# Routing of the third and fourth batch placed between the first units of a mixture-of-experts feed-forward

## The chip, the cores and the metric

The kernel runs on one core of a Trainium2 chip. The metric is the device time of one execution in microseconds; the time shown for a kernel is the median of its runs. The engines are TensorE (PE, matmuls), VectorE (DVE), ScalarE (ACT), GpSimd (POOL) and the sync engine (SP), which here issues most DMAs. Each engine has its own queue of instructions, which it works in order; engines wait for one another by semaphores (`wait_ge(semaphore, value)`, `then_inc(semaphore, 1)`).

## The reference

The input x is 4 batches of 512 tokens with 128 channels. Four blocks follow, each added to x with a tanh gate: a dynamic-time-warping alignment with a context, a first feed-forward, attention to the context, a second feed-forward. The change lies in the first feed-forward, a mixture of 64 experts of width 64 with 8 chosen for each token:

```python
logits = jnp.einsum('bsh,he->bse', hidden_states, router_w)
affinity = jax.nn.sigmoid(logits)
top_scores, top_idx = jax.lax.top_k(affinity, K)                       # K = 8
top_w = top_scores / (jnp.sum(top_scores, axis=-1, keepdims=True) + 1e-09)
...
shared = jnp.einsum('bsi,ih->bsh', jax.nn.silu(hidden_states @ shared_gate_w) * (hidden_states @ shared_up_w), shared_down_w)
...
expert_act = jax.nn.silu(gate_out) * up_out
routed = jnp.einsum('bsei,eih->bsh', expert_act * router_mask[..., None], expert_down_k)
return shared + routed
```

## The kernel before

**Tiling.** The program works with the hidden width on the partitions and the tokens on the free side, a chunk of 512 tokens (one batch) at a time. The experts are taken in 33 groups of 128 rows: group 0 is the shared expert, each further group holds two routed experts. A unit is one group and one chunk; unit u = 4 * group + chunk, so units 0 to 3 are the shared expert (no mask), 4 to 7 group 1, and unit 8 is the first of group 2. Every fp32 operand is split in a high and a low part, and each product is three matmuls of 128x512 (high x high, low x high, high x low).

**One unit.** TensorE makes the gate product (lines 1203 to 1205, tile `bank`, ps[4] or ps[5]) and the up product (same lines, tile `bank_pair`, ps[6] or ps[7]); ScalarE takes the silu of the gate (L1017); VectorE multiplies silu and up (L1901 for the shared expert; L1903 and then L1911, with the mask, for the others) and counts the semaphore `act`; ScalarE rounds the result to act_hi (L1003); GpSimd subtracts it to get act_lo (L803); TensorE makes the down product, L1356 and L1357 with act_hi and L1359 with act_lo. TensorE's order is gate(u), up(u), down(u - 2). Gate(u) waits for the silu of unit u - 2, up(u) for the `act` of unit u - 2 (it overwrites that unit's bank), L1359 for act_lo. ScalarE's order is silu(u), act_hi(u - 1). GpSimd's L803 waits for act_hi. The first three groups are written out in the program, the others run in loops.

**Routing.** For each batch b, TensorE makes the logits and ScalarE the sigmoid (L988, its semaphore `s_score`). VectorE's `route0(b)` finds the 8 best scores of each of the 4 tiles (L1698), their sum (L1700), the scores with the best replaced by 0 (L1702), and the reciprocal of the sum (L1704, L1706); that releases `s_rcp`. GpSimd's `route0(b)` subtracts to leave the 8 chosen scores (L789) and multiplies by the reciprocal (L793, two instructions); that releases `s_sel`. VectorE's `turn0(b)` transposes the weights (L1711) and releases `s_wt`.

**Masks.** The sync queue waits for `s_wt` in `store_masks0(b)` and writes the weights of batch b to DRAM with 4 DMAs (L634). `mask0` reads them back, each row copied to 64 partitions, with 2 DMAs (L610): for group 1 batch by batch, for the later groups all four batches in one pair. The order in its queue is: store 0; then for b = 0 to 3: store b + 1, wait for store b, load the mask of group 1 for batch b; then the pair of group 2 (tile `mask`, buffer 0), which VectorE's L1911 of unit 8 waits for; then a loop that loads the weights of group g and, once all units of group g - 2 are done on VectorE, the mask of group g.

```python
sp.wait_ge(s_upd, B)
store_masks0(0)
for b in range(B):
    if b + 1 < B:
        store_masks0(b + 1)
    sp.wait_ge(s_mst[b], 16 * 4)
    mask0(1, 1, slice(b, b + 1), s_mask1[b])
mask0(2, 0, slice(0, B), FF_MASK[0][0])
```

In the kernel before, VectorE runs route0 of all four batches and turn0 of the first three ahead of unit 0, and turn0(3) ahead of unit 1; GpSimd runs route0 of all four batches ahead of its unit 0. Most of the tiles named here lie in one large tensor, which the profile calls `arena`.

Of the kernel before, what the change touches and what calls it, by code (L numbers as in the profile page):

```python
# [36 lines left out]
def program(nc, x, ctx_1024, g_xattn, g_ffn, r0_w, sg0, su0, sd0, eg0, eu0, ed0,  # L37
            Wq, bq, Wk, bk, Wv, bv, Wo, bo, r1_w, wg1, wu1, wd1, swg1, swu1, swd1, out):
    B, S, H = x.shape
# [83 lines left out]
    with ctx:  # L123
# [229 lines left out]
        def mask_loaded(half):  # L353

            return 16 * MASK_DMAS * half

        def products(f, u):

            return u - CHUNKS * SHARED[f]
# [324 lines left out]
        def _(pool):  # L684
# [100 lines left out]
            def route0(b):  # L785

                tiles = slice(TPB * b, TPB * (b + 1))
                pool.wait_ge(s_rcp, b + 1)
                nc.gpsimd.tensor_tensor(rest[0][:, tiles, :], aff[0][:, tiles, :], rest[0][:, tiles, :],  # L789
                                        ALU.subtract).then_inc(s_dif, 1)  # L790
                pool.wait_ge(s_dif, b + 1)
                for k in range(2):
                    ins = nc.gpsimd.tensor_tensor(wsel[0][:, b, TPB * k:TPB * (k + 1), :], rest[0][:, tiles, 32 * k:32 * (k + 1)],  # L793
                                                  rsum[:, 2, tiles].unsqueeze(2).broadcast_to([P, TPB, 32]), ALU.mult)
                ins.then_inc(s_sel, 1)

            def feed_forward(f):
                def unit(g, k):
                    u = CHUNKS * g + k
                    pool.wait_ge(FF[f]["ahi"], u + 1)  # L800
                    if not (isinstance(g, int) and u < 2):
                        pool.wait_ge(FF[f]["down"], u - 1)
                    nc.gpsimd.tensor_tensor(act_lo[:, k % 2, :], act_a[:, k % 2, :], act_hi[:, k % 2, :].bitcast(F32),  # L803
                                            ALU.subtract).then_inc(FF[f]["alo"], 1)

                for u in range(CHUNKS * PEEL):
                    if f == 0 and u == 0:
                        for b in range(B):
                            route0(b)
                    unit(u // CHUNKS, u % CHUNKS)  # L810
                with pool.Fori(0, LOOPS[f]) as t:
                    for u in range(BODY * CHUNKS):
                        unit(BODY * t + PEEL + u // CHUNKS, u % CHUNKS)
                for u in range(CHUNKS * (GROUPS[f] - REST), CHUNKS * GROUPS[f]):
                    unit(u // CHUNKS, u % CHUNKS)

            norm(1)
            feed_forward(0)
            norm(2)
            attention()  # L820
            norm(3)
            feed_forward(1)


# [605 lines left out]
        def _(dve):  # L1430
            steps = [0]

            def done(ins):

                steps[0] += 1
                ins.then_inc(s_dve, 1)
                return steps[0]

            def after(step):

                dve.wait_ge(s_dve, step)
# [38 lines left out]
            def low(k, b):  # L1480
                dve.wait_ge(s_xhi, B * k + b + 1)
                nc.vector.tensor_tensor(xn_lo[:, sl(b)], xT[:, sl(b)], xn_hi[:, sl(b)].bitcast(F32),
                                        ALU.subtract).then_inc(s_xlo, 1)
# [209 lines left out]
            def route0(b):  # L1693

                tiles = slice(TPB * b, TPB * (b + 1))
                dve.wait_ge(s_score, b + 1)
                for t in range(TILES)[tiles]:
                    best = done(nc.vector.max(top8[:, t, :], aff[0][:, t, :]))  # L1698
                after(best)
                total = done(nc.vector.tensor_reduce(rsum[:, 0, tiles], top8[:, tiles, :], AX_X, ALU.add))  # L1700
                for t in range(TILES)[tiles]:
                    done(nc.vector.match_replace(rest[0][:, t, :], top8[:, t, :], aff[0][:, t, :], 0.0))  # L1702
                after(total)
                total = done(nc.vector.tensor_scalar(rsum[:, 1, tiles], rsum[:, 0, tiles], 1e-9, None, ALU.add))  # L1704
                after(total)
                nc.vector.reciprocal(rsum[:, 2, tiles], rsum[:, 1, tiles]).then_inc(s_rcp, 1)  # L1706

            def turn0(b):

                dve.wait_ge(s_sel, b + 1)  # L1710
                nc.vector.transpose(wT[0][:, b].rearrange("p t c -> p (t c)"),  # L1711
                                    wsel[0][:, b].rearrange("p t c -> p (t c)")).then_inc(s_wt, 1)
# [170 lines left out]
            def feed_forward(f):  # L1883
                def split_lo(g, j):

                    dve.wait_ge(FF[f]["whi"], g + 1)
                    nc.vector.tensor_tensor(w_lo[:, j, :], w_raw[:, j, :], w_hi[:, j, :].bitcast(F32),  # L1887
                                            ALU.subtract).then_inc(FF[f]["wlo"], 1)

                def unit(g, k, j, half, last=False):  # L1890
                    u = CHUNKS * g + k
                    i = k % 2
                    early = isinstance(g, int) and u < 2
                    if k == SPLIT_AT and not last and not (isinstance(g, int) and g == 0):
                        split_lo(g + 1, 1 - j)
                    dve.wait_ge(FF[f]["silu"], u + 1)
                    dve.wait_ge(FF[f]["up"], u + 1)
                    if isinstance(g, int) and g < SHARED[f]:
                        if not early:
                            dve.wait_ge(FF[f]["alo"], u - 1)  # L1900
                        nc.vector.tensor_tensor(act_a[:, i, :], act_s[:, i, :], ps[6 + i][:], ALU.mult).then_inc(FF[f]["act"], 1)  # L1901
                        return
                    nc.vector.tensor_tensor(ps[6 + i][:], act_s[:, i, :], ps[6 + i][:], ALU.mult).then_inc(FF[f]["t"], 1)  # L1903
                    if f == 0 and isinstance(g, int) and g == 1:
                        dve.wait_ge(s_mask1[k], 16 * MASK_DMAS)
                    elif k == 0:
                        dve.wait_ge(FF_MASK[f][j], mask_loaded(half))
                    dve.wait_ge(FF[f]["t"], products(f, u + 1))
                    if not early:
                        dve.wait_ge(FF[f]["alo"], u - 1)  # L1910
                    nc.vector.tensor_tensor(act_a[:, i, :], ps[6 + i][:], mask[:, j, 512 * k:512 * (k + 1)],  # L1911
                                            ALU.mult).then_inc(FF[f]["act"], 1)

                for g in range(PEEL):
                    for k in range(CHUNKS):
                        u = CHUNKS * g + k
                        if f == 0 and u == 0:

                            route0(0)
                            for b in range(1, B):  # L1920
                                route0(b)
                                turn0(b - 1)
                        if f == 0 and u == 1:
                            turn0(B - 1)
                        if f == 1 and u == 2:
                            low(3, B - 1)
                        if f == 1 and u in ROUTE1_BEFORE:
                            for part, step in ROUTE1_BEFORE[u]:
                                route1(part, step)
                        unit(g, k, g % 2, g // 2)  # L1930
                with dve.Fori(0, LOOPS[f]) as t:
                    for i in range(BODY):
                        for k in range(CHUNKS):
                            unit(BODY * t + PEEL + i, k, (PEEL + i) % 2, BODY // 2 * t + (PEEL + i) // 2)
                for g in range(GROUPS[f] - REST, GROUPS[f]):
                    for k in range(CHUNKS):
                        unit(g, k, g % 2, g // 2, last=g == GROUPS[f] - 1)

            norm(1, add_aligned)
            feed_forward(0)  # L1940
            norm(2, add_ffn(0))
            attention()
            feed_forward(1)
            for n in range(CHUNKS):
                add_ffn(1)(n)
# [26 lines left out]
```

## Time and profile before

| | |
|---|---|
| median of 3 runs | 762.02 us (761.12 to 763.22) |
| profiled execution | 759.99 us, span 758.3 us |
| busy, share of span | PE 87%, DVE 75%, ACT 52%, POOL 46% |
| first feed-forward's units | from about 146 us to about 430 us |
| mean granted TensorE clock | 0.903 of full speed |

The span runs from the first to the last recorded instruction of the profiled execution. PE is TensorE's matmuls, and the sync queue is shown as SPq. In a timeline, the figure in brackets is the time that the engine stood idle before the instruction, followed by what released it. Busy shares are means over all stages; what an edit is worth is read in its own stage.

### The profile page before, as it was taken

What the parts mean: (1) busy time and instruction counts of PE and PEld (TensorE: products, weight loads), DVE (VectorE), ACT (ScalarE), POOL (GpSimd) and SP (SyncE); (2) the same over time, 40 slices, a digit from 0 to 9 for tenths busy, and PEclk for the clock granted to TensorE, in tenths of its full rate; (3) what the DMA queues carried; (4) which work ended last, traced back from release to release, by engine and by line L of the source; (5) the groups of instructions that cost most, each with busy time, mean ns of one, the idle gap of its engine ahead of it and who ended that gap; (6) DMA issues with size and microseconds to landing.
All of it is one profiled execution on the core that took longest, in us unless ns stands there. A gap on an engine that the chain in (4) does not pass through costs nothing.

```text
span 758.3 us, 13278 instructions
## 1 busy us (share of the span) xinstructions
PE 656.2 (87%) x3528; PEld 502.7 (66%) x3528; DVE 570.3 (75%) x1608; ACT 397.4 (52%) x707; POOL 349.5 (46%) x326
## 2 busy tenths in 40 slices
PE   5329523889999999999999779988989999999997
PEld 2116313667888888888888546655768888888885
DVE  6579895857777777777777784889867777777775
ACT  4624220555655655565556544544456555655654
POOL 4000130565666666666666560000356666666664
PEclk9855555699999999999999968998799999999999
DMA  6565543067776776677677100000166656665761
GB/s 155 76 86 169 166 131 62 7 147 151 161 145 139 159 154 141 146 157 154 135 154 158 28 2 2 2 2 13 38 122 153 151 133 160 156 144 138 159 153 56
DMA packets 85148, 86.50 MB, mean 114 GB/s; under 512 B 41109, under 2 KB 65294, under 8 KB 82166
## 3 DMA queue, kind: packets, MB, share of 16 engines
q1 hardware_dynamic: 77340, 79.80, 49.4%
q10 hardware_dynamic: 7769, 6.25, 3.1%
q8 instruction: 17, 0.28, 0.1%
q14 instruction: 22, 0.17, 0.1%
HBM read 76.84 MB, written 9.17 MB: 113 GB/s over the span
## 4 chain that ended last, share of the span: by engine, by line
PE 71%; DVE 12%; DMA 5%; issue 4%; SPq 4%; ACT 2%; POOL 2%; ACTq 1%; DVEq 0%; POOLq 0%
PE bank L1203 7%; PE bank L1204 7%; PE bank_quad L1359 7%; PE bank L1205 7%; PE bank_pair L1203 7%; PE bank_quad L1356 7%; PE bank_pair L1204 7%; PE bank_pair L1205 7%; PE bank_quad L1357 7%; DMA scr_d<-arena 3%; PE bank_pair L1252 2%; PE bank L1295 2%; DVE arena L1670 1%; PE bank_pair L1175 1%; DVE rden L1799 1%
## 5 line engine op out<-in xcount | busy, mean ns | idle before, releaser
L803 POOL TENSOR_TENSOR act_lo<-arena,act_hi 128x512 fp32r<-128x512 f32 x232 | 300.3, 1294 | 191.2 <-ACT act_hi L1003 147.7
L1017 ACT ACTIVATE arena<-bank 128x512 f32<-128x512 f32 x232 | 138.8, 598 | 183.3 <-PE bank L1205 183.3
L1903 DVE TENSOR_TENSOR bank_pair<-arena,bank_pair 128x512 f32<-128x512 f32 x220 | 152.4, 693 | 99.9 <-ACT arena L1017 70.6
L1911 DVE TENSOR_TENSOR arena<-bank_pair,arena 128x512 f32<-128x512 f32 x220 | 152.1, 691 | 17.8 <-DMA arena<-scr_mask 5.7
L1003 ACT ACTIVATE act_hi<-arena 128x512 fp32r<-128x512 f32 x232 | 144.5, 623 | 14.4 <-DVE arena L1901 7.5
L1359 PE MATMUL bank_quad<-act_lo,w_hi 128*128 128x512 f32 x232 | 93.0, 401 | 4.0 <-POOL act_lo L803 4.0
L1203 PE MATMUL bank_pair<-xn_hi,w_hi 128*128 128x512 f32 x232 | 92.8, 400 | 3.5 <-DVE arena L1911 1.8
L1203 PE MATMUL bank<-xn_hi,w_hi 128*128 128x512 f32 x232 | 93.1, 401 | 0.0
L1204 PE MATMUL bank<-xn_hi,w_lo 128*128 128x512 f32 x232 | 93.1, 401 | 0.0
L1356 PE MATMUL bank_quad<-act_hi,w_hi 128*128 128x512 f32 x232 | 93.0, 401 | 0.0
L1204 PE MATMUL bank_pair<-xn_hi,w_lo 128*128 128x512 f32 x232 | 92.1, 397 | 0.0
L1357 PE MATMUL bank_quad<-act_hi,w_lo 128*128 128x512 f32 x232 | 91.4, 394 | 0.0
L1205 PE MATMUL bank<-xn_lo,w_hi 128*128 128x512 f32 x232 | 91.4, 394 | 0.0
L1205 PE MATMUL bank_pair<-xn_lo,w_hi 128*128 128x512 f32 x232 | 91.3, 394 | 0.0
L748 POOL TENSOR_SCALAR xn<-x_res,mv,rstd 128x128 f32<-128x128 f32 x16 | 14.1, 884 | 116.5 <-DVE rstd L1466 81.5
L1175 PE MATMUL bank_pair<-ident,prep_in 128*128 128x128 f32 x75 | 21.6, 425 | 41.2 <-ACT prep_out L953 30.5
L1359 PEld LDWEIGHTS bank_quad<-act_lo,w_hi 128*128 128x128 f32 x232 | 43.7, 189 | 18.1 <-POOL act_lo L803 7.1
L1203 PEld LDWEIGHTS bank_pair<-xn_hi,w_hi 128*128 128x128 f32 x232 | 44.1, 190 | 15.8 <-DVE arena L1911 2.6
L1887 DVE TENSOR_TENSOR w_lo<-w_raw,w_hi 128x384 fp32r<-128x384 f32 x54 | 52.4, 970 | 0.0
L1203 PEld LDWEIGHTS bank<-xn_hi,w_hi 128*128 128x128 f32 x232 | 44.3, 191 | 11.0 <-issue 1.9
L1204 PEld LDWEIGHTS bank<-xn_hi,w_lo 128*128 128x128 f32 x232 | 44.3, 191 | 10.4
L1205 PEld LDWEIGHTS bank_pair<-xn_lo,w_hi 128*128 128x128 f32 x232 | 44.2, 190 | 10.6
(252 smaller groups left out, 981.1 us busy)
## 6 DMA issues: line engine op xcount, KB each, us to landing
arena<-scr_mask SPq DMA_DIRECT2D x94, 512.0 KB, 6.6
scr_w<-prep_out ACTq DMA_DIRECT2D x25, 192.0 KB, 2.4
w_raw<-scr_w SPq DMA_DIRECT2D x25, 192.0 KB, 6.3
w_raw<-in_L_ffn_expert_gate_k SPq DMA_DIRECT2D x32, 64.0 KB, 5.9
w_raw<-in_L_ffn_expert_up_k SPq DMA_DIRECT2D x32, 64.0 KB, 5.6
w_raw<-in_L_ffn_expert_down_k SPq DMA_DIRECT2D x64, 32.0 KB, 5.3
prep_in<-in_L_ffn_wg SPq DMA_DIRECT2D x21, 64.0 KB, 2.0
prep_in<-in_L_ffn_wu SPq DMA_DIRECT2D x21, 64.0 KB, 2.4
```

The lines of the kernel that those rows point to most:

```text
L803: nc.gpsimd.tensor_tensor(act_lo[:, k % 2, :], act_a[:, k % 2, :], act_hi[:, k % 2, :].bitcast(F32), ALU.subtract).then_inc(FF[f]["alo"], 1)
L1003: nc.scalar.activation(act_hi[:, j, :], act_a[:, j, :], ACT.Copy).then_inc(FF[f]["ahi"], 1)
L1017: nc.scalar.activation(act_s[:, k % 2, :], ps[4 + k % 2][:], ACT.Silu).then_inc(FF[f]["silu"], 1)
L1203: nc.tensor.matmul(out, w_h, x_h, start=start, stop=False)
L1204: nc.tensor.matmul(out, w_l, x_h, start=False, stop=False)
L1205: return nc.tensor.matmul(out, w_h, x_l, start=False, stop=stop)
L1356: nc.tensor.matmul(ps[n][:], w_hi[:, j, DOWN:DOWN + P], act_hi[:, i, :], start=first, stop=False)
L1357: nc.tensor.matmul(ps[n][:], w_lo[:, j, DOWN:DOWN + P], act_hi[:, i, :], start=False, stop=False)
L1359: nc.tensor.matmul(ps[n][:], w_hi[:, j, DOWN:DOWN + P], act_lo[:, i, :], start=False, stop=last).then_inc(FF[f]["down"], 1)
L1887: nc.vector.tensor_tensor(w_lo[:, j, :], w_raw[:, j, :], w_hi[:, j, :].bitcast(F32), ALU.subtract).then_inc(FF[f]["wlo"], 1)
L1903: nc.vector.tensor_tensor(ps[6 + i][:], act_s[:, i, :], ps[6 + i][:], ALU.mult).then_inc(FF[f]["t"], 1)
L1911: nc.vector.tensor_tensor(act_a[:, i, :], ps[6 + i][:], mask[:, j, 512 * k:512 * (k + 1)], ALU.mult).then_inc(FF[f]["act"], 1)
```

## The change

VectorE: ahead of unit 0 stand only route0(0), route0(1) and turn0(0). Ahead of unit 1 stand route0(2) and turn0(1), ahead of unit 2 route0(3) and turn0(2), ahead of unit 3 turn0(3). GpSimd: ahead of unit 0 stand route0(0) and route0(1), ahead of unit 1 route0(2), ahead of unit 2 route0(3). No instruction, tile, semaphore or DMA is added or removed, and the programs of TensorE, ScalarE and the sync engine stay as they are.

```diff
@@ GpSimd, feed_forward
                 for u in range(CHUNKS * PEEL):
-                    if f == 0 and u == 0:
-                        for b in range(B):
+                    if f == 0 and u < B - 1:
+                        for b in (range(2) if u == 0 else (u + 1,)):
                             route0(b)
                     unit(u // CHUNKS, u % CHUNKS)
@@ VectorE, feed_forward
                         if f == 0 and u == 0:
-
                             route0(0)
-                            for b in range(1, B):
-                                route0(b)
-                                turn0(b - 1)
-                        if f == 0 and u == 1:
-                            turn0(B - 1)
+                            route0(1)
+                            turn0(0)
+                        if f == 0 and 1 <= u < B:
+                            if u + 1 < B:
+                                route0(u + 1)
+                            turn0(u)
```

## Rows read from the trace of the kernel before

**Rows 1.** The page: chain that ended last, shares of the span by engine.

```profile
PE 71%; DVE 12%; DMA 5%; issue 4%; SPq 4%; ACT 2%; POOL 2%; ACTq 1%; DVEq 0%; POOLq 0%
```

**Rows 2.** TensorE's timeline, 138 to 182 us: start, length, line, tiles, [idle before, releaser].

```profile
148.67 0.63 PE L1205 MATMUL bank_pair<-xn_lo,w_hi 128*128 128x512 f32 x1
...
151.08 0.39 PE L1203 MATMUL bank<-xn_hi,w_hi 128*128 128x512 f32 x1
...
153.68 0.50 PE L1203 MATMUL bank_pair<-xn_hi,w_hi 128*128 128x512 f32 x1 [1.76 <-DVE arena L1901]
...
155.71 0.51 PE L1359 MATMUL bank_quad<-act_lo,w_hi 128*128 128x512 f32 x1 [0.60 <-POOL act_lo L803]
...
162.31 0.39 PE L1203 MATMUL bank<-xn_hi,w_hi 128*128 128x512 f32 x1
...
170.66 0.39 PE L1203 MATMUL bank<-xn_hi,w_hi 128*128 128x512 f32 x1
...
174.52 0.39 PE L1203 MATMUL bank<-xn_hi,w_hi 128*128 128x512 f32 x1
```

**Rows 3.** Waits, 140 to 175 us (total, times, longest); last the sync queue's.

```profile
DVE arena L1911 <- DMA arena<-scr_mask: 2.6, 1, 2.6
...
SPq L634 <- DVE arena L1711: 0.2, 1, 0.2
```

**Rows 4.** Timeline of VectorE, 120 to 215 us, same columns.

```profile
148.43 0.41 DVE L1711 STREAM_TRANSPOSE arena<-arena 128x256 f32<-128x256 f32 x1
148.77 0.56 DVE L1698 MAX8 arena<-arena 128x8 f32<-128x64 f32 x4
...
150.53 0.42 DVE L1711 STREAM_TRANSPOSE arena<-arena 128x256 f32<-128x256 f32 x1
...
152.98 0.65 DVE L1901 TENSOR_TENSOR arena<-arena,bank_pair 128x512 f32<-128x512 f32 x1
154.40 0.45 DVE L1711 STREAM_TRANSPOSE arena<-arena 128x256 f32<-128x256 f32 x1 [0.77 <-POOL arena L793]
...
171.40 0.69 DVE L1911 TENSOR_TENSOR arena<-bank_pair,arena 128x512 f32<-128x512 f32 x1 [2.57 <-DMA arena<-scr_mask]
```

**Rows 5.** Timeline of GpSimd, 138 to 182 us.

```profile
152.80 0.72 POOL L789 TENSOR_TENSOR arena<-arena 128x256 f32<-128x256 f32 x1 [0.53 <-DVE arena L1706]
153.60 0.76 POOL L793 TENSOR_TENSOR arena<-arena 128x128 f32<-128x128 f32 x2
154.37 1.28 POOL L803 TENSOR_TENSOR act_lo<-arena,act_hi 128x512 fp32r<-128x512 f32 x1
```

**Rows 6.** Timeline of ScalarE, 138 to 182 us.

```profile
150.58 0.60 ACT L1017 ACTIVATE arena<-bank 128x512 f32<-128x512 f32 x1 [1.62 <-PE bank L1205]
```

**Rows 7.** The sync queue's timeline, 138 to 182 us, issues merged.

```profile
148.92 3.85 SPq L634 DMA_DIRECT2D scr_mask<-arena  x8
152.82 1.11 SPq L610 DMA_DIRECT2D arena<-scr_mask  x2
...
156.12 2.10 SPq L610 DMA_DIRECT2D arena<-scr_mask  x2
...
160.38 3.75 SPq L610 DMA_DIRECT2D arena<-scr_mask  x6
```

**Rows 8.** The same, narrow stretches at 150.8, 156.7 and 163.8 us.

```profile
150.98 0.32 SPq L634 DMA_DIRECT2D scr_mask<-arena  x1
...
156.64 1.59 SPq L610 DMA_DIRECT2D arena<-scr_mask  x1
...
163.51 0.62 SPq L610 DMA_DIRECT2D arena<-scr_mask  x1
```

**Rows 9.** DMAs issued at 161.0 and 163.6 us: KB, us to landing.

```profile
arena<-scr_mask SPq DMA_DIRECT2D x1, 128.0 KB, 3.3
...
arena<-scr_mask SPq DMA_DIRECT2D x1, 512.0 KB, 7.9
```

**Rows 10.** One stretch: busy PE, PEld, DVE, ACT, POOL; clock, DMA share, GB/s.

```profile
240.00:280.00 40.00, 40.00 (x174) 32.21 (x173) 30.54 (x44) 23.40 (x43) 24.96 (x20) 1.00 0.73 147
```

## The prediction

> **What bounds the kernel now.** The first view to read is the chain of work that ended last [rows 1]: 71% of the span lies on TensorE, so a microsecond moves the end only where TensorE waits for it. Inside the loop of the first feed-forward there is no such wait: a stretch of 40 us shows TensorE busy for 40.00 us [rows 10]. A delay at the loop's entry is therefore never made up in it, and a gain there would be kept. The change touches only that entry, 144 to 158 us, so the timelines of that stretch come next.
>
> TensorE there works through steps. Step u is the gate product of unit u, its up product, and the down product of unit u - 2 (nine matmuls, then the next step). The first matmuls (L1203) of steps 6 and 10 start at 162.31 and 170.66, so a step takes (170.66 - 162.31) / 4 = 2.09 us [rows 2]. Three things interrupt this rhythm [rows 2]. The up product of step 2 waits 1.76 us, to 153.68, because it overwrites a bank that VectorE's unit 0 must have read. The down product of unit 0 waits 0.60 us for GpSimd's act_lo. And step 11 starts at 174.52 instead of at 170.66 + 2.09 = 172.75, 1.77 us late. This third loss begins on VectorE: its multiplication by the mask of group 2 (unit 8) waits 2.57 us for the DMA of the mask, to 171.40 [rows 4], the only DMA wait of any engine in this stretch [rows 3]. The first two losses are what routing costs at the entry; the third is the price of the masks that routing produces.
>
> **Why both are one question.** VectorE's transpose turn0(b) ends the routing of batch b, and the sync queue stores the batch right after it. The queue starts at 148.92, just behind turn0(0) at 148.43 [rows 4, 7]. Its fifth store starts at 150.98, when turn0(1), started at 150.53 and 0.42 long, has ended; the queue waited only 0.2 us for it [rows 3, 4, 8]. From then on it is a row of issues almost without a gap up to 163.51, where the second half of the mask of group 2 is issued [rows 7, 8]; that half lands 7.9 us later, at 171.4 [rows 9], where VectorE's wait ends. The queue's own issuing carries the length from 150.98 to 171.4, so whatever delays the fifth store delays the landing.
>
> **The change, part 1: VectorE's unit 0 comes earlier.** No instruction is added or removed and no DMA is moved in the program. Unit 0 (L1901) now follows turn0(0). It needs the up product, whose last matmul starts at 148.67 and takes 0.63 [rows 2]; so it starts at 149.4 instead of 152.98 and ends at 150.0 [rows 4]. TensorE's up product of step 2 needs it at 151.8, so the 1.76 us go.
>
> What is late next is GpSimd. ScalarE's act_hi of unit 0 stands behind its silu of unit 1 (150.58, 0.60 long [rows 6]), so it runs from 151.1 to 151.7, and act_lo of unit 0 runs on GpSimd from 151.8 to 153.05 (1.28 [rows 5]). Without the gap TensorE reaches that point at 152.9 and waits 0.2. Then GpSimd works its own queue in order. A route0 costs it from 152.80 to 153.60 + 0.76 = 154.36, so 1.56 us [rows 5]. Route0(2) takes it to 154.6, act_lo of unit 1 to 155.9, route0(3) to 157.5, act_lo of unit 2 to 158.8. TensorE wants act_lo of unit 1 at 155.3 and of unit 2 at 158.2: two waits of 0.7. Step 2 starts at 151.08 [rows 2], before any of this; four steps take 8.36 us, the three waits 1.6, and the refilling of the pipeline after each some 0.1, which puts step 6 at 161.3 instead of 162.31. The entry alone gains 1.0 us.
>
> **Part 2: VectorE's routing comes later.** Route0(2) started at 148.77 and its turn0(1) at 150.53, 1.76 later [rows 4]. It now starts behind unit 0, at 149.95. Turn0(1) starts at 151.7 and ends at 152.15, and the fifth store starts at 152.2 instead of 150.98: 1.2 us later. The next stores, those of batch 2, follow four stores and two mask loads: from 150.98 to the end of those loads at 152.82 + 1.11 = 153.93 are 2.95 us [rows 7, 8], so the queue is free for them at 155.15. Turn0(2) must wait for GpSimd's route0(2), to 154.65, and ends at 155.05, 0.1 ahead of that. Turn0(3) stands behind GpSimd's route0(3) at 157.5 and ends at 157.95; the queue wants it four stores and two loads later (4 x 0.48 + 2.10 [rows 7]), at 159.2. Both keep pace, so the queue is 1.2 us late throughout. VectorE itself waits 1.8 us for that last transpose, as it already waits 0.77 for it now [rows 4]; unit 3 behind it ends at 158.6, and the up product of step 5 wants it at 159.9. This costs nothing.
>
> **Part 3: where the two meet.** The masks of group 1 come first. The second half of batch 2's pair lands 3.3 us after its issue [rows 9], at 164.2 now and at 165.4 after. Unit 6, ready at 164.1 by the earlier start, must wait for it, and its act_lo then ends at 168.2, where TensorE wanted it at 167.4: 0.9 of the 1.0 us gained is gone before step 9. By that reckoning step 10 starts at 170.7, as before the change. Then the mask of group 2 lands at 171.4 + 1.2 = 172.6. Everything behind it (the second product of unit 8, act_hi, act_lo, step 11) is the same chain as now, 1.2 us later. In the loop there is nothing to take it back [rows 10], and the later stages start from its end. Sum: +1.2 us. The profiled execution took 759.99 us (span 758.3 and 1.7 around it) and would become 761.2; the median of the runs, 762.02, becomes 763.2.
>
> **The unknown in it.** The queue's delay need not reach the landing in full. One issue, at 156.64, took 1.59 us where the six later ones take 3.75 / 6 = 0.62 each [rows 7, 8]: 1.0 us in which the queue stood. If that comes from descriptors piled up by the thirteen issues ahead of it, a pause of 1.2 us drains the pile and the landing moves by 0.2; if it belongs to that place in the program, by 1.2; at worst it comes twice, 2.2. I take 1.2, since the issues around it show no growing length. From below nothing makes the landing earlier than now. The page "Perfetto Trace Analysis" of the Trainium skill, section "DMA Instruction — HWDGE (DVE, Sync)", says that such an instruction's profiled time is the waiting for the descriptor generator and the generating, which may outrun the descriptor buffer; that fits the long issue, and by it the small value would be the right one.
>
> The mask of group 3 is issued behind that of group 2, once unit 7 is done on VectorE, and unit 7 is not as much later as the masks: the distance between the two shrinks by at most 1.2 us. If transfers shared the engines evenly, that would hold the mask of group 2 back by half of it, 0.6 us more. The Trainium skill, page "DMA: Bandwidth & Descriptors", section "Queues, rings and completion order", has each DMA engine consume a queue's descriptors in ring order, so one issued later could not hold it back; by that rule this cost is nothing, and the two halves' landings here do not decide it.
>
> **The rivals.** (A) The forecast, +1.2: 763.2.
> (B) The pile drains: the mask of group 2 lands at 171.6. For it speaks the one long issue; against it that no issue ahead of it was stretched. 762.02 + 0.2 = 762.2.
> (C) The entry's gain is kept, 761.0: the masks would have to land over 1 us earlier than I place them, or the 2.57 us wait would have to be another's than the mask's. Against it: the landing of the issue at 163.51 and the end of the wait are both 171.4.
> (D) The other side, slower by more than can be overlooked: GpSimd falls behind. Turn0(2) has only 0.1 us ahead of the sync queue, and GpSimd's route0(2) stands behind act_lo of unit 0 in its queue. From 0.1 us of lateness on, each microsecond goes through store, mask and step 11 in full. If GpSimd is one act_lo (1.29) later than I reckon, turn0(2) and turn0(3) both are, and the time is 762.02 + 1.2 + 1.3 = 764.5. Against it: GpSimd's operations have shown steady lengths beside VectorE's work.
>
> **How the numbers follow.** Chances: A 0.60, B 0.17, C 0.08, D 0.10; 0.05 for what I do not see, on either side. A change below 0.3% (2.3 us) is about what a measurement of this kernel can't tell from none. A, B and C lie within it, D beyond it. So faster 0.05, same 0.83, slower 0.12. The range reaches from C to a little beyond D: 760.9 to 765.0.
>
> **What would show it.** In the profile after: L1901 of unit 0 at 149.4 and no 1.76 us wait of TensorE at 153.7; instead three short waits at L1359 for act_lo at 153, 156 and 159; step 6 at 161.3. The fifth store at 152.2 with a wait of 1.4 us of the sync queue for L1711. VectorE's wait for the mask of group 2 ending at 172.6, and step 11 at 175.7. If step 6 is at 161.3 and step 11 not later than 174.5, part 2 was wrong; if the fifth store is at 152.2 but the landing is not 1.2 later, the queue had slack (B). The prediction as a whole is wrong if step 11 moves by something other than the landing of that mask.

## The result and the profile after

| | before | after |
|---|---|---|
| median of 22 runs each | 759.04 us | 761.35 us |
| profiled execution, span | 759.99, 758.3 us | 761.41, 759.7 us |
| first MAX8 of the routing | 144.74 | 144.20 |
| step 6 of TensorE, from that MAX8 | 17.57 | 16.44 |
| step 11 of TensorE, from that MAX8 | 29.78 | 31.01 |

The ratio of the times is 1.0022 (95% interval 1.0012 to 1.0033): the change costs 0.22% or 1.7 us, between 0.9 and 2.5. The two executions reach the first feed-forward 0.54 us apart, so every time below is counted from VectorE's first MAX8 of the routing (144.74 before, 144.20 after); a time "at 16.4" is meant so. By the two medians alone the loss would be 2.3 us; the text goes by the ratio, which has the interval.

TensorE's timeline of the kernel after, to be read against [rows 2]:

```profile
160.64 0.39 PE L1203 MATMUL bank<-xn_hi,w_hi 128*128 128x512 f32 x1
...
169.57 0.39 PE L1203 MATMUL bank<-xn_hi,w_hi 128*128 128x512 f32 x1
...
172.85 0.50 PE L1203 MATMUL bank_pair<-xn_hi,w_hi 128*128 128x512 f32 x1 [2.42 <-DVE arena L1911]
...
175.21 0.40 PE L1203 MATMUL bank<-xn_hi,w_hi 128*128 128x512 f32 x1
```

Step 6 is 1.1 us earlier than before, step 10 (at 25.4) still 0.6, and then TensorE stands 2.42 us for VectorE's L1911 of unit 8, where it stood 0.64 before. Step 11 is 1.23 us later. VectorE's timeline, to be read against [rows 4], shows the early unit and what delays the routing behind it:

```profile
148.74 0.69 DVE L1901 TENSOR_TENSOR arena<-arena,bank_pair 128x512 f32<-128x512 f32 x1 [0.43 <-PE bank_pair L1205]
...
150.85 1.02 DVE L1704 TENSOR_SCALAR arena<-arena 128x4 f32<-128x4 f32 x1
...
152.01 0.41 DVE L1711 STREAM_TRANSPOSE arena<-arena 128x256 f32<-128x256 f32 x1
...
154.42 0.62 DVE L1704 TENSOR_SCALAR arena<-arena 128x4 f32<-128x4 f32 x1
...
172.10 0.69 DVE L1911 TENSOR_TENSOR arena<-bank_pair,arena 128x512 f32<-128x512 f32 x1 [4.68 <-DMA arena<-scr_mask]
```

Unit 0 stands where it was forecast (4.5 against 4.7), and the wait for group 2's mask has grown from 2.57 to 4.68 us. New is L1704, an addition of a constant to four numbers for each partition: 1.02 and 0.62 us where it took 0.16 for these batches before. GpSimd's timeline tells what ran beside it:

```profile
150.56 1.30 POOL L803 TENSOR_TENSOR act_lo<-arena,act_hi 128x512 fp32r<-128x512 f32 x1 [0.93 <-ACT act_hi L1003]
...
153.74 1.28 POOL L803 TENSOR_TENSOR act_lo<-arena,act_hi 128x512 fp32r<-128x512 f32 x1
```

150.85 + 1.02 = 151.87 against 150.56 + 1.30 = 151.86; 154.42 + 0.62 = 155.04 against 153.74 + 1.28 = 155.02. Each time L1704 ends with GpSimd's act_lo. The kernel before has a weak sign of the same: its addition for batch 1 takes 0.27 us and ends with GpSimd's multiplications L793, 148.03 + 0.27 = 148.30 against 147.52 + 0.75 = 148.27.

```profile
148.03 0.27 DVE L1704 TENSOR_SCALAR arena<-arena 128x4 f32<-128x4 f32 x1
```

```profile
147.52 0.75 POOL L793 TENSOR_TENSOR arena<-arena 128x128 f32<-128x128 f32 x2
```

So turn0(1) starts at 7.8 instead of the 7.0 forecast, and the fifth store follows. The sync queue, against [rows 7]:

```profile
148.38 5.87 SPq L634 DMA_DIRECT2D scr_mask<-arena  x8
...
157.56 1.11 SPq L610 DMA_DIRECT2D arena<-scr_mask  x2
...
160.84 3.75 SPq L610 DMA_DIRECT2D arena<-scr_mask  x6
```

The eight first stores take 5.87 us instead of 3.85, and the fifth starts at 8.25 instead of 6.24: 2.0 us late, not 1.2. But the pair of loads that took 2.10 before takes 1.11 now, so the last six loads start at 16.64 instead of 15.64, only 1.0 late. The long issue is not gone. It is now the third store of batch 0, ahead of the queue's wait for turn0(1), where it costs nothing:

```profile
149.27 1.62 SPq L634 DMA_DIRECT2D scr_mask<-arena  x1
```

```profile
SPq L634 <- DVE arena L1711: 1.2, 2, 1.1
```

What makes an issue long can be read too. The DMA view has one packet on the queue named instruction in each of the two places, first before (156.7 to 157.0), then after (149.4 to 149.7):

```profile
q8 instruction: 1, 0.02, 21.8%
```

```profile
q8 instruction: 1, 0.02, 22.1%
```

The packet has 16 KB. It lasts from 156.78 to 157.83 before and from 149.52 to 150.58 after, and the long issue ends 0.4 and 0.3 us behind it. All 16 profiles of this case have exactly one long issue and one such packet between the first store and the last of these loads, and in all 16 the issue ends 0.3 to 0.4 us behind the packet. So an issue of the sync queue stands until that packet has come, by the queue's name a piece of the program. This rests on the timing alone, as no run moved the packet, and what sets its moment stays open.

The wait for the mask ends 27.90 - 26.66 = 1.24 us later, and step 11 is as much later. Of this the issues explain 1.0; the mask's second half lands 8.1 us behind its issue where it took 7.9 before.

### The profile page after: what moved, and what is told of

It reads as the page before. It is cut to its first block, busy times and chain, and to the rows that moved or that the text cites. A ratio compares the mean times of both kernels' runs of the same rounds, so it can differ in the third digit from the quotient of the medians.

```text
span 759.7 us, 13278 instructions
## 1 busy us (share of the span) xinstructions
PE 660.5 (87%) x3528; PEld 504.8 (66%) x3528; DVE 570.9 (75%) x1608; ACT 397.9 (52%) x707; POOL 350.2 (46%) x326
## 4 chain that ended last, share of the span: by engine, by line
PE 69%; DVE 15%; issue 5%; DMA 4%; SPq 4%; ACT 1%; POOL 1%; ACTq 0%; DVEq 0%; POOLq 0%
PE bank L1203 7%; PE bank L1204 7%; PE bank_quad L1359 7%; PE bank L1205 7%; PE bank_pair L1203 7%; PE bank_quad L1356 7%; PE bank_pair L1204 7%; PE bank_pair L1205 6%; PE bank_quad L1357 6%; PE bank_pair L1252 2%; PE bank L1295 2%; DMA scr_d<-arena 1%; DVE arena L1670 1%; DVE rden L1799 1%; DMA scr_on<-arena 1%
## 5 line engine op out<-in xcount | busy, mean ns | idle before, releaser
L803 POOL TENSOR_TENSOR act_lo<-arena,act_hi 128x512 fp32r<-128x512 f32 x232 | 300.8, 1297 | 192.4 <-ACT act_hi L1003 149.2
L1911 DVE TENSOR_TENSOR arena<-bank_pair,arena 128x512 f32<-128x512 f32 x220 | 152.1, 691 | 21.5 <-DMA arena<-scr_mask 9.5
L1359 PE MATMUL bank_quad<-act_lo,w_hi 128*128 128x512 f32 x232 | 93.3, 402 | 5.0 <-POOL act_lo L803 5.0
L1359 PEld LDWEIGHTS bank_quad<-act_lo,w_hi 128*128 128x128 f32 x232 | 43.7, 189 | 20.4 <-POOL act_lo L803 9.6
```

The costliest lines, as they stand in the source:

```text
L1359: nc.tensor.matmul(ps[n][:], w_hi[:, j, DOWN:DOWN + P], act_lo[:, i, :], start=False, stop=last).then_inc(FF[f]["down"], 1)
```

## The experiments

All ratios are against runs of the kernel before on the same chip; microseconds are the ratio's, times 759. The landmarks come from one profiled execution each, and carry chance of their own, above all by the place of the long issue.

**Masks out of the way, in both kernels.** The loads of groups 1 and 2 read a row of ones, ahead of the stores:

```diff
...
+            for b in range(B):
+                ones0(1, slice(b, b + 1), s_mask1[b])
+            ones0(0, slice(0, B), FF_MASK[0][0])
             store_masks0(0)
...
-                mask0(1, 1, slice(b, b + 1), s_mask1[b])
-            mask0(2, 0, slice(0, B), FF_MASK[0][0])
```

> The kernel before, with the masks of groups 1 and 2 read from a row of ones, all issued before the first store (the routed weights of these two groups are left out; the stores still happen). Times are counted from VectorE's first MAX8 of the routing: before, step 6 starts at 17.6, step 11 at 29.8. Theory (the landing of group 2's mask sets step 11): VectorE waits for no mask, step 11 at 17.6 + 5 x 2.09 = 28.0, the whole 1.8 us faster than before. Rival (something else than the mask holds step 11, the wait is only attributed to it): step 11 stays at 29.8 and the time is within 0.5 us.

> The changed kernel, with the same masks of ones. Theory (the change gains 1.1 us for TensorE at the entry, and only the later masks take it back): step 6 at 16.4 as in the changed kernel, step 11 at 16.4 + 10.45 = 26.9, some 2.9 us faster than before and 1.1 faster than the kernel before with masks of ones. Rival (the new order costs TensorE time itself, by GpSimd's act_lo behind its routing): not faster than the kernel before with masks of ones.

Measured: 0.9975 (0.9961 to 0.9990), 1.9 us faster, and 0.9960 (0.9946 to 0.9974), 3.0 us faster. TensorE's step 11, first with the order of before (MAX8 at 143.21), then with that of after (MAX8 at 143.69):

```profile
171.20 0.39 PE L1211 MATMUL bank<-xn_hi,w_hi 128*128 128x512 f32 x1
```

```profile
170.53 0.39 PE L1211 MATMUL bank<-xn_hi,w_hi 128*128 128x512 f32 x1
```

That is 27.99 and 26.84. So the mask's landing costs the kernel before 1.8 us, and with the masks out of the way the changed order is 1.15 us better by these two profiles, 1.1 us by the runs (whose two intervals overlap). Part 1 of the forecast and its size are right, and the sign turns only by the masks.

**The late store alone.** The kernel before, only the sync queue's store of batch 1 held back to turn0(2) (shown), or to turn0(3) (4 in place of 3):

```diff
-                sp.wait_ge(s_wt, b + 1)
+                sp.wait_ge(s_wt, 3 if b == 1 else b + 1)
```

> The kernel before; only the sync queue's store of batch 1 waits until turn0(2) is done instead of turn0(1), so the fifth store starts at 8.3 us from the first MAX8 instead of 6.2, where the changed kernel has it too (8.2). The compute engines' order is that of before. Theory (the change loses by the late fifth store alone): step 6 at 17.6 as before, the mask of group 2 lands 1.0 to 2.1 us later, step 11 at 30.8 to 31.9, the time 1.0 to 2.1 us over before. Rival (the store's lateness is absorbed by the queue; the change loses by its order on the engines): step 11 at 29.8, time as before.

> The same with a larger dose: the store of batch 1 waits for turn0(3), the fifth store starts at 10.1 from the first MAX8, 3.9 later than before. Theory (one for one, less what the one long issue of 1.59 us gives back): the mask of group 2 lands 2.9 to 3.9 later, step 11 at 32.7 to 33.7, time 2.9 to 3.9 us over before. Rival (the landing is bound by the transfer rate, not by the issues): less than 1.5 later.

VectorE's L1911 of unit 8, for the dose of 2.1 us (MAX8 at 143.59) and of 3.9 us (MAX8 at 143.23):

```profile
171.43 0.69 DVE L1911 TENSOR_TENSOR arena<-bank_pair,arena 128x512 f32<-128x512 f32 x1 [3.76 <-DMA arena<-scr_mask]
```

```profile
172.92 0.69 DVE L1911 TENSOR_TENSOR arena<-bank_pair,arena 128x512 f32<-128x512 f32 x1 [4.64 <-DMA arena<-scr_mask]
```

The wait ends at 27.84 and 29.69 against 26.66, so 1.2 and 3.0 us later; step 11 is at 30.94 and 32.80, 1.2 and 3.0 later, with step 6 unmoved (17.55 and 17.57). In these profiles the late store alone, without any change in the order on the compute engines, makes step 11 as late as the whole change does. It is not one for one. The smaller dose has its long issue in the stores of batch 2 and its last loads start 1.9 us late, but the mask lands 7.2 us behind its issue instead of 7.9; the larger one has the long issue hidden ahead of the fifth store, as the kernel after has.

The times missed both theories and rivals: 1.0054 (1.0038 to 1.0071) and 1.0072 (1.0046 to 1.0097), 4.1 and 5.5 us, where 1.0 to 2.1 and 2.9 to 3.9 were expected. They are four runs each, and the profiled execution of the smaller dose was the fastest of its four (759.58 beside 762.48 to 763.35 us). What those slower executions have more, no profile shows; it stays open.

**The early unit alone.** VectorE's unit 0 behind turn0(1), so that nothing on VectorE delays the fifth store:

```diff
-                    if f == 0 and u < B - 1:
-                        for b in (range(2) if u == 0 else (u + 1,)):
+                    if f == 0 and u < 2:
+                        for b in (range(3) if u == 0 else (3,)):
...
                             route0(1)
                             turn0(0)
-                        if f == 0 and 1 <= u < B:
-                            if u + 1 < B:
-                                route0(u + 1)
-                            turn0(u)
+                            route0(2)
+                            turn0(1)
+                        if f == 0 and u == 1:
+                            route0(3)
+                            turn0(2)
+                        if f == 0 and u == 2:
+                            turn0(3)
```

> The part of the change that does not touch the fifth store: VectorE's unit 0 stands behind route0(2) and turn0(1) (GpSimd: act_lo of unit 0 behind route0(2)), route0(3) and turn0(2) ahead of unit 1, turn0(3) ahead of unit 2. Theory (the loss comes from the late masks only, the early unit is a gain that the mask wait swallows): the fifth store at 6.2 from the first MAX8 as before, step 6 at 16.4 to 16.8 (before 17.6), step 11 at 29.8 to 30.4, the time from 0 to 0.6 us over before. Rival (the new order costs by itself): time as the changed kernel, 1.2 or more over before.

Measured: 1.0012 (0.9999 to 1.0026), step 6 at 16.58, step 11 at 30.28. Both landmarks are in the theory's ranges. The time, 0.9 us (-0.1 to 2.0), does not tell the theory (0 to 0.6) from the rival (1.2 or more), nor this kernel from the one after. The fifth store was not at 6.2 but at 7.37: here too the third store of batch 0 was the long issue (1.75 us), and too long to end in time. For all that, the wait for the mask ended at 26.92, only 0.26 us later than before; L1704 of batch 3, held again for 0.62 us, has no part in this, as the queue was not yet free when its transpose ended. The other half of step 11's lateness lies behind that wait, where the profile shows something new:

```profile
171.91 0.50 PE L1203 MATMUL bank_pair<-xn_hi,w_hi 128*128 128x512 f32 x1 [1.83 <-DVE arena L1911]
...
172.50 0.63 PE L1205 MATMUL bank_pair<-xn_lo,w_hi 128*128 128x512 f32 x1
...
173.94 0.80 PE L1359 MATMUL bank_quad<-act_lo,w_hi 128*128 128x512 f32 x1
```

The same stretch by the windows view (busy time of PE, PEld, DVE, ACT, POOL, then granted clock, DMA share, GB/s), first in this kernel, then in the kernel after:

```profile
171.00:177.00 6.00, 5.09 (x14) 3.58 (x15) 4.51 (x7) 3.12 (x6) 2.57 (x2) 0.72 1.04 184
```

```profile
171.00:177.00 6.00, 3.55 (x14) 2.45 (x15) 4.08 (x7) 3.06 (x6) 2.58 (x2) 1.00 1.08 198
```

The granted clock is 0.72 over this stretch: it falls to the lower of its levels (1.2 instead of 2.4 GHz), and a matmul takes 0.63 instead of 0.40 us; from the end of VectorE's wait to step 11 it takes 3.36 instead of 3.12 us, and from step 11 to step 12 2.71 instead of 2.09. That is a loss of 0.9. The Trainium skill, page "TensorE: Matmul & The Clock Gate", section "Part 1: The HAM clock gate (the "warmup" mystery)", has TensorE's clock set by how busy TensorE has been. The trace agrees in that the fall follows a wait of 1.83 us; but the kernel after waited 2.42 us at the same place and kept its clock, so a wait alone does not tell.

**L1704 and GpSimd.** The addition left out, and (shown) its result in PSUM:

```diff
-                total = done(nc.vector.tensor_scalar(rsum[:, 1, tiles], rsum[:, 0, tiles], 1e-9, None, ALU.add))
+                denom = ps[3][:, 480 + TPB * b:480 + TPB * (b + 1)] if b >= 2 else rsum[:, 1, tiles]
+                total = done(nc.vector.tensor_scalar(denom, rsum[:, 0, tiles], 1e-9, None, ALU.add))
```

> The changed kernel without VectorE's addition of 1e-9 to the sum of the scores (L1704 is left out), which took 1.02 us for batch 2 and 0.62 for batch 3, ending each time when GpSimd's act_lo ended, against 0.16 and 0.27 otherwise. Theory A (that instruction alone cannot run beside GpSimd's): the reciprocal runs beside act_lo at its 0.18 us, turn0(1) and the fifth store come 0.9 to 1.1 us earlier. Theory B (any instruction at this place, also the reciprocal, waits until GpSimd is done): the reciprocal takes about 1.0 and the fifth store is at most 0.3 earlier. Group 2's mask would land up to 1.0 earlier by A, step 11 at 30.0 to 31.0 from the first MAX8, instead of 31.0.

> The changed kernel, with the output of L1704 (and the input of the reciprocal) in PSUM instead of SBUF for batches 2 and 3; nothing left out. Theory A (VectorE's form with source and result in SBUF needs what GpSimd's two-input subtraction holds): L1704 takes 0.15 to 0.3 us for batches 2 and 3 though act_lo runs beside it. Theory B (its length is a matter of place or of a semaphore, not of the operands): 1.0 and 0.6 as in the changed kernel.

They do not answer the question for act_lo: in their profiles TensorE's clock rose later, act_hi came later, and act_lo of unit 0 started only when the addition's place was past (151.00, where the reciprocal had started at 150.72, and 151.39, where it had started at 151.29). In the first of them the reciprocal of batch 3 ran inside GpSimd's L793 (153.22 inside 153.06 to 153.46) at its 0.17 us, so not every VectorE instruction at this place is held. The times were 1.0025 (1.0012 to 1.0037) and 1.0023 (1.0008 to 1.0039). Step 11 missed the expected 30.0 to 31.0, with 31.67 and 31.58. The fifth store was 0.7 to 0.9 us earlier than in the kernel after, and yet the last six loads started at 16.70 and 16.65 as there, since the long issue now lay in the row (+0.8 and +0.7); and both mask waits of TensorE (2.27 and 2.65 us) ended with the clock at half. So the addition was done eight times, to be sure of the overlap:

```diff
+                for n in range(8):
...
+                        total = done(nc.vector.tensor_scalar(denom, rsum[:, 0, tiles], 1e-9, None, ALU.add))
```

> The changed kernel with VectorE's addition of 1e-9 done eight times in a row for batches 2 and 3 (source and results in SBUF), so that some of them surely meet GpSimd's act_lo, which in earlier versions sometimes started before and sometimes after that instruction. Theory A (a VectorE instruction of this form cannot start while GpSimd's two-input subtraction runs): the eight take 8 x 0.16 us plus a stretch of up to 1.3 us that ends when act_lo ends; one of them is shown at 0.5 to 1.3 us. Theory B (the 1.02 us were something else): all eight at 0.16 to 0.3 us beside act_lo.

> The same eight additions with their results in PSUM (source in SBUF). Theory A with operands (only source and result both in SBUF collide): all at 0.15 to 0.3 us, whether act_lo runs or not. Theory A without operands (any VectorE instruction that reads SBUF collides): one of them again 0.5 to 1.3 us, until act_lo ends.

With the results in SBUF, GpSimd's act_lo, then VectorE's eight additions, and the first of them in a narrow stretch:

```profile
150.15 1.29 POOL L804 TENSOR_TENSOR act_lo<-arena,act_hi 128x512 fp32r<-128x512 f32 x1 [0.87 <-ACT act_hi L1004]
```

```profile
150.45 1.51 DVE L1708 TENSOR_SCALAR sums<-arena 128x4 f32<-128x4 f32 x8
```

```profile
150.45 1.02 DVE L1708 TENSOR_SCALAR sums<-arena 128x4 f32<-128x4 f32 x1
```

With the results in PSUM:

```profile
149.63 1.28 POOL L803 TENSOR_TENSOR act_lo<-arena,act_hi 128x512 fp32r<-128x512 f32 x1 [1.15 <-ACT act_hi L1003]
```

```profile
149.85 0.60 DVE L1707 TENSOR_SCALAR bank_quad<-arena 128x4 f32<-128x4 f32 x8
```

In SBUF the first of the eight is held from 150.45 until act_lo ends at 151.44 and the other seven pass in 0.5 us. In PSUM all eight pass in 0.60 us inside act_lo (149.63 to 150.91), and again for batch 3. Theory A with its operands holds. These two kernels were executed once each, so they tell nothing about the time. This is what the Trainium skill, page "SBUF — State Buffer", section "Who interferes with whom", has as an exclusive lock: a VectorE instruction in a two-port mode and a GpSimd instruction share a pair of ports, and whichever starts first keeps the other out for its whole length. The trace agrees: 1.02 us for an instruction that takes 0.16 us alone, with act_lo started first.

**Loads by batch.** Both kernels, computing everything, with group 2's mask in four pairs of 128 KB loads, each pair with its own semaphore, and group 3's weights ahead of the stores:

```diff
             raw0(2, 0)
+            sp.wait_ge(FF[0]["wlo"], 2)
+            raw0(3, 1)
...
-            mask0(2, 0, slice(0, B), FF_MASK[0][0])
+            for b in range(B):
+                mask0(2, 0, slice(b, b + 1), s_dst[b])
...
+                    elif f == 0 and isinstance(g, int) and g == 2:
+                        dve.wait_ge(s_dst[k], 32 + 16 * MASK_DMAS)
```

> The kernel before, computing everything, with the mask of group 2 loaded batch by batch (eight loads of 128 KB, each with its own semaphore, in place of two of 512 KB) so that unit 8 waits only for batch 0, and the weights of group 3 loaded before the stores instead of behind the masks. Theory (the landing of group 2's mask costs TensorE 1.8 us): VectorE's wait of 2.6 us is gone, step 11 at 28.0 from the first MAX8, time 1.8 us below before. Rival (the loads are bound by transfer rate and land late batch by batch too): step 11 not before 29.

> The changed kernel with the same two edits of the loads. Theory: TensorE leads by 1.1 us at step 6, the masks of group 1 (batches 2 and 3, VectorE waits 1.4 and 0.4 us for them in the changed kernel) take most of it back, 0.6 to 0.9; step 11 at 27.5 to 28.0, time 1.8 to 2.4 us below before, thus as fast as the kernel before with these loads or up to 0.5 faster. Rival (the change is worse by itself even with the mask of group 2 early): 0.5 us or more slower than the kernel before with these loads.

> That order, computing everything, with the loads of e7_before_split (group 2's mask batch by batch, group 3's weights ahead of the stores). Theory: nothing swallows the early unit now; no mask wait of over 0.5 us, TensorE never idle for over 1 us at the entry, so its clock does not fall as it did behind the 2.6 us gap in that kernel; step 11 at 26.9 to 27.6 from the first MAX8, time 2.3 to 3.0 us below before. Rival (late masks of group 1 take it back as in the changed kernel): step 11 at 27.5 to 28.0, 1.8 us below before.

| order on the engines | ratio | waits for masks, groups 1 and 2 | step 6 | step 11 |
|---|---|---|---|---|
| before | 0.9982 (0.9970 to 0.9995) | none | 18.99 | 29.42 |
| after | 0.9977 (0.9964 to 0.9990) | 0.24, 1.47 | 16.42 | 27.52 |
| unit 0 behind turn0(1) | 0.9971 (0.9958 to 0.9983) | 0.35 | 16.57 | 27.00 |

The 2.6 us wait for group 2's mask is gone in all three. The second meets its step 11 and has 0.6 us more between steps 14 and 15. The last one meets its step 11 too and, with 2.2 us under before (1.3 to 3.2), comes just short of the expected 2.3 to 3.0 (a wait of 0.67 us for group 3's mask is left behind this stretch). Its interval is clear of both the kernel before and the kernel after; the three rows of this table are not clear of one another, so by the times the gain is that of the loads, and what the order adds is shown by the landmarks alone. The first one missed its step 11 by 1.4 us, for a reason that its profile shows. TensorE's clock rose early there (3.9), TensorE waited 2.58 us at the entry for VectorE's unit 0, which both other orders do not have, and behind that wait the clock fell. (So its 29.42 meets the rival's "not before 29" by the number and not by the cause.) Its time, 1.4 us under before, and that of the second, 1.7, were expected at 1.8 and at 1.8 to 2.4.

```profile
152.15 0.50 PE L1212 MATMUL bank_pair<-xn_hi,w_hi 128*128 128x512 f32 x1 [2.58 <-DVE arena L1910]
...
154.17 0.80 PE L1368 MATMUL bank_quad<-act_lo,w_hi 128*128 128x512 f32 x1 [0.59 <-POOL act_lo L812]
154.76 0.63 PE L1212 MATMUL bank<-xn_hi,w_hi 128*128 128x512 f32 x1
```

**The missing half microsecond: clock or queue?** The changed kernel with filler matmuls in the wait, and the changed kernel once more on the same chip:

```diff
+                    for _ in range(2 if f == 0 and isinstance(g, int) and u == 10 else 0):
+                        three_pass(ps[4 + k % 2][:], w_hi[:, j, 0:P], w_lo[:, j, 0:P], xn_hi[:, tok], xn_lo[:, tok])
```

> The changed kernel with six more matmuls on TensorE in step 10 (the gate product of unit 10 made three times, the last one counts), 1.4 us of work that falls into the 2.4 us in which TensorE waits there for the mask of group 2. Theory (what the changed kernel loses beyond the 1.2 us of the landing is TensorE's clock, which in e3_no_add, e4_psum, e10_mid, e11_add8 and e12_add8_psum fell to half behind this wait and cost 0.6 to 0.9 us): no matmul of 0.63 us behind the wait, step 13 two plain steps behind step 11, time 0 to 0.6 us below the changed kernel's. Rival (the clock has no part, the fall is chance whatever TensorE does): a fall in the profile again, or a time above the changed kernel's by up to 1.4.

> The changed kernel once more, on the same chip as e13_after_fill, as its measure. Theory: the fifth store between 7.2 and 8.3 us from the first MAX8, step 11 at 31 +- 0.6, and, since the wait at step 10 is over 1.8 us, the clock more likely than not at half behind it: then step 13 at 36 instead of 35.3. Rival: as in its first profile, no fall, step 13 at 35.3.

Measured: 1.0020 (1.0007 to 1.0034) with the filler, 1.0022 (1.0006 to 1.0038) without. There was no fall of the clock in either profile, though TensorE waited 2.1 us in the second. So the filler decides nothing, and the fall that was expected for the second did not come; its fifth store (8.40) and its step 11 lie 0.1 beyond their expected ranges. The second profile of the changed kernel shows instead a later mask (MAX8 at 145.76): the addition, the stores of batch 2 and the mask:

```profile
152.54 1.05 DVE L1704 TENSOR_SCALAR arena<-arena 128x4 f32<-128x4 f32 x1
...
174.34 0.69 DVE L1911 TENSOR_TENSOR arena<-bank_pair,arena 128x512 f32<-128x512 f32 x1 [4.72 <-DMA arena<-scr_mask]
```

```profile
157.33 2.69 SPq L634 DMA_DIRECT2D scr_mask<-arena  x4
...
163.36 3.75 SPq L610 DMA_DIRECT2D arena<-scr_mask  x6
```

The stores of batch 2 take 2.69 us where the first profile has 1.91, the last six loads start at 17.60 (before 15.64), L1911 at 28.58 and step 11 at 31.68: 1.9 us later than before. That points to the queue for the half microsecond, though two profiles don't prove it. The fifth store is 2.0 and 2.2 us late in the two. In the first, the long issue lay ahead of the wait for turn0(1) and cost nothing, where the kernel before pays 1.0 us for it; by that luck the addition's 0.86 us did not show in the landing. In the second it lay in the stores of batch 2 (+0.8) and was paid. Two profiles with 1.2 and 1.9 us have a mean of 1.6, the runs say 1.7.

## Why the prediction was right or wrong

The median of 761.35 us lies in the range, in part by luck: the range was built on 762.02 us for the kernel before, the median of three runs, and 22 runs put that kernel at 759.04. The sum is the fairer measure, and its +1.2 us lies in the measured interval (0.9 to 2.5). The conclusion was wrong: it called the change no change, with 0.12 for a loss, and the loss is clear of noise. Two steps failed. The step from the sum to the chances took 2.3 us for the least that can be told, where the runs told 1.7 us with 0.8 to each side. And in the sum the term of part 2, the fifth store's lateness, was put at 1.2 us and measured 2.0 and 2.2.

- *Part 1, the early unit.* Right. Unit 0 at 4.54 (forecast 4.7), step 6 at 16.44 (16.6). The waits for act_lo came at L1359, the first 0.2 and the others 0.59 each (forecast 0.2 and 0.7); the masks-out-of-the-way pair puts the part's worth at 1.15 us.
- *Part 2, VectorE's routing later.* The mechanism was right (the fifth store, shown alone by the landmarks of the late-store kernels); its size was not. The term was 1.2 us; the fifth store came 2.0 us later, and 2.2 in the second profile. Behind it stands the tacit step that a moved instruction keeps its length beside new neighbours. Route0(2) was costed by its 1.76 us of before [rows 4], when no act_lo ran beside it; beside GpSimd's L803 its addition costs 0.86 more. The prediction looked only at GpSimd's lengths ("steady lengths beside VectorE's work") and not at VectorE's, though the 0.27 us of batch 1's addition stood in the trace of before. The queue waited 1.1 us for turn0(1) where 1.4 was forecast, as the long issue filled part of the time.
- *Turn0(2) keeps pace by 0.1 us.* It missed by about that much: it ended at 11.38, the queue was free at 11.21. Turn0(3) kept pace. Rival D had the right place and not the cause: GpSimd's route0(2) was done at 9.55 (forecast 9.9), and VectorE, held twice, came to the transpose only at 10.97. D's price of another act_lo was not paid.
- *Part 3, where the two meet.* Right as a mechanism: VectorE waited 1.41 and 0.44 us for group 1's masks of batches 2 and 3, which took back 0.6 us of the lead (0.9 forecast), and step 11 hangs on the landing of group 2's mask.
- *The long issue.* The prediction left open whether it drains (B), stays, or comes twice. It came once in every profile, in changing places, and each time it ended just behind a 16 KB packet of the instruction queue. So the runs do not bear out a pile of descriptors, nor the small value that the prediction drew from it. (From the fifth store on, eleven issues lie ahead of it, not thirteen.) In the pair of profiles it fell out of the row and hid the addition, so the measured 1.24 against 1.2 was a hit of two errors.
- *Rivals.* B (+0.2) and C (-1.0) are out by the interval, and by both profiles of the changed kernel.
- *The chances.* A forecast of +1.2 us was put wholly under "no change" because a bound of 2.3 us was taken for what can be told. With 22 runs the interval is 0.8 us to each side. A gain and a loss that nearly cancel should not have been read as a flat case, as most of the unknown terms lay on the side of loss.

## What to carry to other kernels

Before work is moved off an engine's critical stretch, follow what it releases: here the moved transposes start a row of 22 DMA issues, each issued behind the last, and the gain of 1.1 us on TensorE is paid at the end of that row. A moved instruction has to be costed beside its new neighbours, here VectorE's addition from SBUF to SBUF beside GpSimd's subtraction. Where both ends matter, move only what nothing hangs on (here unit 0 behind turn0(1)), which alone gained nothing (1.0012), and loosen what the wait really needs (one batch of the mask, not four): together 2.2 us under the kernel before, of which the loads alone gave 1.4 (the two intervals overlap). And before one profile's landmark is believed to half a microsecond, find the long issue in it and see whether it lies in the row that counts.

## What the runs showed of the hardware

- A VectorE addition of 128x4 numbers from SBUF to SBUF is held until a running GpSimd subtraction ends (1.02 us for 0.16); with its result in PSUM it is not (8 in 0.60 us).
- TensorE's clock fell to half after waits of 1.8 to 2.9 us in six of the profiles (five at the mask, one at the entry), and not after waits of 1.6 to 2.4 us in four others at the mask; when it fell, the next step took 0.5 to 1.2 us more. What decides between them stays open.
- TensorE's clock rises at a different moment of the entry in each execution: the first full-speed matmul (0.39 to 0.40 us) starts between 3.8 and 6.5 us from the first MAX8. With VectorE's order of the change this goes with what happens to the addition: where the clock rose by 4.7, act_lo of unit 0 started at 6.1 to 6.6, ahead of the addition (six profiles, among them both of the changed kernel); where it rose at 6.0 or later, at 7.1, behind it (three profiles).
- One issue of the sync queue in this stretch takes 0.7 to 1.5 us more than its kind, in all 16 profiles, in changing places. It ends 0.3 to 0.4 us behind a packet of 16 KB on the DMA queue named instruction, the only one there. It is paid where it falls into the row of issues and costs nothing where it falls ahead of a wait. What sets its moment stays open.
- From the issue of the second half of group 2's mask, loaded in two pieces of 512 KB, to the end of VectorE's wait it took 7.2 to 8.5 us in eleven profiles, without a change of the load.
